# Row and column attention over a 128x192 map: attention times V of all twelve heads as one last stage, with V, x and the result moved in rows of 768 bytes

## What is computed

```
n    = group_norm(x)                        # 32 groups of 6 channels, over the whole map
sw   = softmax over rows of (n[row 0] Wq_s) . (n Wk_s)      # a weight per row, column and head
Q    = n Wq * scale * sw ;  K = n Wk ;  V = n Wv
QK   = einsum('rihd,rjhd->hij', Q, K)       # 192 x 192 per head, summed over rows and d
attn = softmax(QK, axis=j)                  # masks are applied before both softmaxes
out  = x + einsum('hij,rjhd->rihd', attn, V)
```

## Time and profile before

| | |
|---|---|
| median of 3 runs | 582.6 us (578.11 to 585.08) |
| profiled execution, span | 583.2 us |
| busy: PE / DVE / ACT / POOL | 516.6 / 394.4 / 313.4 / 243.0 us |
| mean granted TensorE clock | 0.947 |
| DMA | 183447 packets, 134.30 MB, 230 GB/s over the span |
| packets under 512 bytes | 168224 |

### The profile page before, as it was taken

The page is one execution under the profiler, slowest core; times in us unless marked ns, Lnnn a source line. Parts: engine busy times, 40 slices in busy tenths (PEclk is TensorE's granted clock), DMA queues, the critical chain, the costliest instruction groups (busy, mean ns, idle before and its releaser), DMA issues.

```text
span 583.2 us, 13858 instructions
## 1 busy us (share of the span) xinstructions
PE 516.6 (89%) x5167; PEld 390.0 (67%) x5167; DVE 394.4 (68%) x989; ACT 313.4 (54%) x646; POOL 243.0 (42%) x280
## 2 busy tenths in 40 slices
PE   7697685799999999999899996694999979999893
PEld 5687542355555555455499985494999979998783
DVE  3599767577878777778836686372467663667873
ACT  4477665597999999995412130332456650223231
POOL 2000231755777777774300033572455660002583
PEclk9898899699999999999999999698899998999997
DMA  8997012444666666787699999988777739999998
GB/s 327 384 417 268 2 55 108 163 145 128 217 217 218 215 202 209 200 211 161 120 286 270 269 297 312 320 226 246 256 254 251 258 96 241 303 286 278 309 258 230
DMA packets 183447, 134.30 MB, mean 230 GB/s; under 512 B 168224, under 2 KB 170080, under 8 KB 183392
## 3 DMA queue, kind: packets, MB, share of 16 engines
q1 hardware_dynamic: 132384, 113.80, 63.2%
q10 hardware_dynamic: 51008, 19.76, 13.3%
HBM read 76.92 MB, written 56.62 MB: 229 GB/s over the span
## 4 chain that ended last, share of the span: by engine, by line
PE 68%; DVE 14%; DMA 7%; POOL 3%; ACT 2%; ACTq 2%; issue 2%; SPq 1%; POOLq 0%; DVEq 0%
PE PS L1175 23%; PE PS L1183 13%; PE PS L1271 7%; DVE EXTRA L765 5%; DMA EXTRA<-in_x 4%; PE PS L1301 3%; PE PS L1305 3%; PE PS L1304 3%; PE PS L1303 3%; PE PS L1302 3%; DVE BIG L1040 3%; ACTq L739 2%; POOL BIG L514 2%; DMA out_x<-EXTRA 1%; PE PS L1136 1%
## 5 line engine op out<-in xcount | busy, mean ns | idle before, releaser
L1175 PE MATMUL PS<-WP,EXTRA 128*128 128x384 f16 (+1 forms) x1152 | 159.9, 291 | 8.0 <-DMA EXTRA<-xt_scratch 8.0
L1175 PEld LDWEIGHTS PS<-WP,EXTRA 128*128 128x128 f16 x1152 | 99.3, 99 | 54.9 <-issue 18.8
L514 POOL TENSOR_TENSOR BIG<-BIG,EXTRA 64x512 f32<-64x512 f32 x36 | 45.1, 1265 | 135.6 <-DVE BIG L1040 111.7
L1271 PE MATMUL PS<-BIG,EXTRA 128*128 128x256 f16 x768 | 89.5, 280 | 12.4 <-ACT EXTRA L745 12.4
L471 POOL TENSOR_TENSOR EXTRA<-BIG,EXTRA 128x512 f16<-128x512 f32 x69 | 81.3, 1180 | 42.4 <-ACT EXTRA L578 34.4
L1271 PEld LDWEIGHTS PS<-BIG,EXTRA 128*128 128x128 f16 x768 | 76.4, 100 | 24.7 <-issue 13.2
L1183 PE MATMUL PS<-WP,EXTRA 64*128 64x384 f16 (+1 forms) x1152 | 90.5, 288 | 0.9 <-DVE EXTRA L904 0.9
L477 POOL TENSOR_TENSOR BIG<-EXTRA,BIG 128x192 f16<-128x192 f32 x96 | 53.6, 559 | 49.4 <-ACT BIG L636 49.4
L1183 PEld LDWEIGHTS PS<-WP,EXTRA 64*128 64x128 f16 x1152 | 44.6, 95 | 30.1 <-issue 18.9
L745 ACT ACTIVATE EXTRA<-PS,small 64x512 f32<-64x512 f32 x48 | 31.3, 682 | 60.8 <-PE PS L1271 19.9
L1040 DVE SCALAR_TENSOR_TENSOR BIG<-PS,small,BIG 128x512 f32<-128x512 f32 x72 | 48.9, 738 | 20.5 <-PE PS L1271 20.5
(11 more groups left out here) (177 smaller groups left out, 953.3 us busy)
## 6 DMA issues: line engine op xcount, KB each, us to landing
EXTRA<-in_x SPq DMA_DIRECT2D x28, 768.0 KB, 8.5
xt_scratch<-EXTRA SPq DMA_DIRECT2D x24, 768.0 KB, 3.4
EXTRA<-xt_scratch SPq DMA_DIRECT2D x24, 768.0 KB, 4.3
v_scratch<-EXTRA SPq DMA_DIRECT2D x32, 384.0 KB, 3.9
BIG<-v_scratch SPq DMA_DIRECT2D x16, 768.0 KB, 6.7
BIG<-in_x SPq DMA_DIRECT2D x12, 768.0 KB, 9.5
out_x<-BIG ACTq DMA_DIRECT2D x12, 768.0 KB, 6.4
v_scratch<-EXTRA SPq DMA_DIRECT2D x32, 192.0 KB, 3.9
```

The lines of the kernel that those rows point to most:

```text
L514: pool.tensor_tensor(o, o, OLOW[j % 3][0:E1, :].rearrange("p (r e) -> p r e", r=RI), ALU.add).then_inc(s_lo[h], 1)
L1175: ins = mm(outs[a], xt[:, t, s, q * P:(q + 1) * P], WP[:, t, w, wc], start=first and j == 0, stop=last and j == 2, skip_group_check=True)
L1271: ins = mm(po[:, :, a, :], stationary, moving, start=j == 0, stop=j == len(terms) - 1)
```

## The change

Attention times V is no longer done per half. PE's order becomes: logits of half 0, second projection, logits of half 1, and then one stage of 96 parts over eight tiles and six pairs of heads each. The attention matrices of all twelve heads are kept (`AT` has 12 instead of 6). DRAM scratch for V holds all heads side by side, so a tile's V is 12288 bytes and 6144 bytes for each of 128 partitions. Rows of x and of the result are 192 float32, 768 bytes. V, x and the result lie in "units" (`V_AT`, `X0_AT`, `X1_AT`), most of them in `BIG`; the 64-partition part of x uses partitions 0 to 63 for even tiles and 64 to 127 for odd ones. All loads and all stores of the stage are issued by SP. V's stores in the first projection become one per chunk for 16 chunks and two per chunk for eight.

The diff, cut to its core:

```diff
-    v1_dram = nc.dram_tensor("v1_scratch", [2, 2, E1, R, EH], fp16, kind="Internal").ap()
+    v0_dram = nc.dram_tensor("v0_scratch", [P, R, 2 * E], fp16, kind="Internal").ap()
+    v1_dram = nc.dram_tensor("v1_scratch", [2, E1, R, E], fp16, kind="Internal").ap()
 
...
+                return EXTRA[:, at_units + (at + 5) * UNIT:at_units + (at + 5 + n) * UNIT]
+            return BIG[:, at * UNIT:(at + n) * UNIT]
+
+        V_AT = (-5, 2, 7, 14, 19, -5, 2, 7)
+        X0_AT = (-2, 5, 10, 17, 22, 0, 5, 19)
+        X1_AT = (0, 12, -2, 14)
+        V0 = [units(at, 2).bitcast(fp16).rearrange("p (r s e) -> p r s e", s=2, e=E) for at in V_AT]
+        V1 = [units(at + 2, 1).bitcast(fp16).rearrange("p (r e) -> p r e", e=E) for at in V_AT]
+        XO = [(units(X0_AT[n], 2).rearrange("p (r e) -> p r e", e=E),
+               units(X1_AT[n // 2], 2)[(n % 2) * E1:(n % 2 + 1) * E1].rearrange("p (r e) -> p r e", e=E))
+              for n in range(NRC)]
...
-                    if c < P // CI:
-                        sp.dma_start(v0_dram[h, c * CI:(c + 1) * CI, :, :].rearrange("i r s -> r i s"),
-                                     VS[c % 2][:, :, h, :, :].rearrange("p i s e -> p i (s e)")
-                                     ).then_inc(s_vs[c % 2], 16)
-                    else:
-                        j0 = c * CI - P
-                        for k in range(2):
-                            sp.dma_start(v1_dram[h, k, j0:j0 + CI, :, :].rearrange("i r s -> r i s"),
-                                         VS[c % 2][:, :, h, k, :]).then_inc(s_vs[c % 2], 16)
+                if c < P // CI:
+                    sp.dma_start(v0_dram[c * CI:(c + 1) * CI, :, :].rearrange("i r s -> r i s"),
+                                 VS[c % 2].rearrange("p i s e -> p i (s e)")).then_inc(s_vs[c % 2], 16)
+                else:
+                    j0 = c * CI - P
+                    for k in range(2):
+                        sp.dma_start(v1_dram[k, j0:j0 + CI, :, :].rearrange("i r s -> r i s"),
+                                     VS[c % 2][:, :, k, :]).then_inc(s_vs[c % 2], 16)
...
-            for h in range(2):
-                if h:
-                    for k in (6, 7):
-                        sp.wait_ge(s_out[k], 32)
-                    for b in range(2, 4):
-                        load_xt(b, b)
-                    with sp.Fori(1, TURNS) as t:
-                        for b in range(4):
-                            sp.wait_ge(s_pj[1], (4 * t + b - 3) * 2)
-                            load_xt(4 * t + b, b)
-                    sp.wait_ge(s_pj[1], NG1)
-                load_x(h, 6)
-                load_x(h, 7)
-                for n in range(NV):
-                    sp.wait_ge(s_qk[h], n + 1)
-                    load_v(h, n)
-                    load_x(h, n)
-                for n in range(NRC - NV):
-                    sp.wait_ge(s_av[h], 2 * closes[n] + 2)
-                    load_v(h, n + NV)
-            for k in range(NRC):
-                sp.wait_ge(s_out[k], 64)
...
+            def load_x(n, t):
+                cols = slice(P, C) if t else slice(0, P)
+                sp.dma_start(XO[n][t], xs[rows(n), cols, :].rearrange("r i e -> i r e")).then_inc(s_xl[t][n], 16)
+
+            def store_out(n):
+                sp.wait_ge(s_ad, 2 * HP * (n + 1) - 1)
+                sp.dma_start(outs[rows(n), 0:P, :].rearrange("r i e -> i r e"), XO[n][0]).then_inc(s_out[0][n], 16)
+                sp.wait_ge(s_lo, HP * (n + 1))
+                sp.dma_start(outs[rows(n), P:C, :].rearrange("r i e -> i r e"), XO[n][1]).then_inc(s_out[1][n], 16)
+
+            with sp.Fori(1, TURNS) as t:
+                for b in range(4):
+                    sp.wait_ge(s_pj[1], (4 * t + b - 3) * 2)
+                    load_xt(4 * t + b, b)
+            sp.wait_ge(s_pj[1], NG1)
+            load_v(0)
+            load_x(0, 0)
+            sp.wait_ge(s_qk[1], 1)
+            load_x(0, 1)
+            load_x(1, 1)
+            sp.wait_ge(s_qk[1], 2)
+            load_v(1)
+            load_x(1, 0)
+            sp.wait_ge(s_qk[1], 3)
+            load_v(2)
+            load_x(2, 0)
+            sp.wait_ge(s_qk[1], 4)
+            load_x(2, 1)
+            load_x(3, 1)
+            sp.wait_ge(s_qk[1], 5)
+            load_v(3)
+            load_x(3, 0)
+            sp.wait_ge(s_qk[1], 6)
+            load_v(4)
+            load_x(4, 0)
+
+            store_out(0)
+            sp.wait_ge(s_av, 2 * HP)
+            load_v(5)
+            store_out(1)
+            sp.wait_ge(s_av, 2 * HP * 2)
+            load_v(6)
+            sp.wait_ge(s_out[0][0], 16)
+            load_x(4, 1)
+            load_x(5, 1)
+            store_out(2)
+            sp.wait_ge(s_av, 2 * HP * 3)
+            load_v(7)
+            for n in range(2):
+                sp.wait_ge(s_out[1][n], 16)
+            load_x(5, 0)
+            sp.wait_ge(s_out[0][1], 16)
+            load_x(6, 0)
+            store_out(3)
+            sp.wait_ge(s_av, 2 * HP * 4)
+            load_x(6, 1)
+            load_x(7, 1)
+            store_out(4)
+            sp.wait_ge(s_av, 2 * HP * 5)
+            load_x(7, 0)
+            for n in range(5, NRC):
+                store_out(n)
+            for n in range(NRC):
+                sp.wait_ge(s_out[0][n], 16)
+                sp.wait_ge(s_out[1][n], 16)
 
         @block.gpsimd
         def _(pool):
...
+                attention_low(h, HALF - 2)
+
+            def add_attended(m):
+                (n, hp), t = BLOCK[m // 2], m % 2
+                if hp == 0:
+                    dve.wait_ge(s_xl[t][n], 16)
+                rows = slice((n % 2) * E1, (n % 2 + 1) * E1) if t else slice(0, P)
+                dve.wait_ge(s_av, m + 1)
+                o = XO[n][t][:, :, hp * 2 * D:(hp + 1) * 2 * D]
+                v.scalar_tensor_tensor(o, PS[rows, attended_bank(m), :].rearrange("p (r e) -> p r e", r=RI),
+                                       mxb[rows, WV:WV + 1], o, ALU.mult, ALU.add).then_inc(s_ad, 1)
+
+            dve.wait_ge(s_ql[0], NG0)
+            for k in range(2):
+                dve.wait_ge(s_vs[k], v_stored(NCH - 2 + k))
+            for b in range(2):
+                v.memset(LG[b][E1:P, 1, :], 0.0)
+            softmax_of_heads(0)
+            evacuate1(0, 0)
+            normalise_logits(0, HALF - 1)
+            for g in range(1, 8):
+                if g == 6:
+                    attention_low(0, HALF - 1)
+                evacuate1(0, g)
...
-                    with pe.Fori(1, TURNS) as t:
-                        project1(t)
-
...
+            def wait_for_banks1(t, g):
+
+                if not isinstance(t, int):
+                    pe.wait_ge(s_kvl[1], 8 * t + g - 3)
+                elif t == 0 and g < 3:
+                    when(pe, s_lr[0], (0, HALF - 1, HALF)[g])
+                elif t == 0:
+                    pe.wait_ge(s_kvl[1], g - 2)
+                elif g == 3:
+                    pe.wait_ge(s_atl[0], HALF)
+                else:
+                    pe.wait_ge(s_kvl[1], (7, 8, 6)[g] if g < 3 else 8 * t + g - 3)
...
+            logits(0)
+            project1(0)
+            project1(1)
+            with pe.Fori(2, TURNS) as t:
+                project1(t)
+            logits(1)
+            for m in range(2 * NB):
+                if m == TRANSPOSED_AT:
+                    transposes(1, HALF - 1)
+                attended(m)
```

492 lines of the change are left out of this document (233 added, 259 removed).

## The result

| | before | after |
|---|---|---|
| median | 583.2 us (578.11 to 585.08, 4 runs) | 597.2 us (591.98 to 600.46, 4 runs) |
| ratio after/before | | 1.026, 95% interval 1.018 to 1.034 |
| profiled execution, span | 583.2 us | 590.3 us |
| DMA | 183447 packets, 134.30 MB | 98200 packets, 134.32 MB |

What follows compares the result with a forecast made beforehand. The prediction took PE and DMA as both near their limits, with DMA setting the new end: 412.5 us to the projection's end + 2.0 idle + 173.3 of transfers + 5.4 of loss = 593.2, forecast 593 us, range 565 to 607.

Steps and rivals of the forecast that it cites:

- Up to the second projection: Kernel start to the end of half 0's logits: fewer V stores save ACT's wait, 1.0 us, so it ends at 334.7 us.
- The second projection: 24 chunks at 73.9 us, 0.9 for the sixth head's transposes, 3.0 for new PE waits; end at 412.5 us.
- Logits of half 1: After the second projection: start 3.2 us later, behind POOL, and take 46.0 us, to 461.7.
- PE alone: Attention times V if DMA kept up: 48 head pairs in 83.9 us, 8.4 behind PE, kernel end at 554.9 us.
- The stage by DMA: V, x and results from 412.5 us on: 2.0 us idle, 173.3 of transfers, 5.4 of loss; end at 593.2 us.
- The price of 64 partitions: Loads and stores on 64 partitions in the DMA stage: 215 GB/s, so 12.6 MB take 58.5 us.
- the line through 384 and 6144 bytes: DMA stage, 128 partitions: 768-byte rows put between 325 and 410 GB/s, at 366, so 25.2 MB take 68.8 us.
- the loss of 5.4 us: DMA stage: extra time on 37.7 MB of loads, scaled from 3.8 us seen before, taken to go with the number of transfers.
- SP's single queue adds nothing: DMA stage: all loads and stores in SP's queue cost no extra time, as a transfer is always ahead; size 0.
- The faster one: Rival for the DMA stage: 768-byte rows move like long ones, 146 to 155 us, kernel at 565 us; chance 0.28.
- The much slower one: Rival: one queue in order at 291 GB/s, stage 194.5 us, kernel 609; or 768-byte rows bring nothing, 603; chance 0.22.
- The signs: What the changed profile would show: projection times, DMA share near 1, PE's stage over 95 us, x's rates, idle slices.

Runs made afterwards that it cites:

- e4: The changed kernel with every load of x for the residual cut to the first of its 16 rows: 565.3 us, stage 154.1 us.
- e2: The changed kernel with x of columns 128 to 191 loaded by 8 rows on 128 partitions instead of 16 on 64: 584.2 us, stage 167.9 us.
- e11: A separate kernel of transfers only, no computation, fourteen phases one behind the other, executed once: some 205 GB/s on either half, 372 or 373 for a load beside a store.
- e3: The changed kernel with each load of x and each store split into two transfers of 384-byte rows: 603.1 us, stage 191.2 us.
- e1: The changed kernel with the stores of the result issued by ACT instead of SP: 584.9 us, stage 171.5 us.

## Why the prediction was right, point by point

The forecast was 593 us (range 565 to 607); the median measured is 597.2. The sum itself ends at 593.2 us on the time axis of a profile; the profiled execution ends at 590.3. Its mechanism, DMA and not PE sets the end, is shown by e4: with 17.7 MB left out the stage is 25.9 us shorter. What the change lost by was in good part another thing than the sum had, the order of SP's queue. That its largest term agrees within 1 us is in part luck, as told below.

- **Up to the second projection: 334.7 forecast, 331.2 measured.** ACT's wait for V's store is gone, and the bound of 1.7 us was nearer than the 1.0 taken. The rest of the 4.5 us lies in the earlier part: in its first 100 us the profiled execution had a clock of 0.96, before 0.93, which no step of the change explains.
- **The second projection: 77.8 us forecast, 79.1 measured.** PE's new waits in the first turn were put at 3.0 us. The view of waits of after (total, times, longest) has 3.1:

```profile
PE PS L1240 <- DVE BIG L1020: 1.7, 1, 1.7
PE PS L1232 <- DVE BIG L1020: 1.4, 2, 0.8
```

  Its end came at 410.3 us, forecast 412.5.
- **Logits of half 1: 3.2 + 46.0 us forecast, 3.2 + 44.5 measured**, at a clock of 1.00 instead of 0.96.
- **PE alone: 554.9 us forecast.** From the end of the projection that is 142.4 us; e4's stage took 154.1, with 90.4 us for the head pairs instead of 83.9, and 16.0 behind PE instead of 8.4. The term was up to 11.7 us too small (part of it are stores that queue in e4). It did not matter, as DMA's end was later.
- **The stage by DMA: 180.7 us forecast, 180.0 measured.** The price of 64 partitions is right: 174 to 236 GB/s in the trace, and e2 puts 12.1 us on half of these transfers, forecast by difference 12.8. The 366 GB/s for 128 partitions is not: one direction shows 328 in after and 326 in e11, and the line through 384 and 6144 bytes does not hold at 768 for a single load. With e11's rates for one direction, 327 and 205 GB/s, and V as forecast the stage would be 2.0 + 77.1 + 61.5 + 46.0 = 186.6 us, an estimate, already without the loss of 5.4 us. It took 6.6 us less, which fits the short stretches in which loads and stores overlap in after too, at some 370 GB/s. So a rate that no single direction has and a loss taken for another reason met the right number. e3 gives the price of row length, together with that of 32 more transfers, as 11.2 us of stage, forecast 10.1.
- **"SP's single queue adds nothing": wrong as a statement on the kernel.** There were few idle slices, as the prediction said, and yet 8.5 us of stage came back when the stores left SP's queue. The step looked only for pauses. What it missed is that one queue in order runs most loads and stores one behind the other, and side by side they move more: 372 GB/s on the same half where each alone has some 205 (e11), and near 370 in e1 where after had 303 in the mean. The sum hid this, as its rates were read from transfers that ran one at a time. The Trainium skill ("DMA: Bandwidth & Descriptors", section "Issuing engines are not separate DMA queues") says that issuing from several engines saves only the time of issue. The run with V in ACT's queue agrees (0.8 us); the run with the stores there does not (8.5 us of stage, with DMA as busy as before).
- **The rivals.** The faster one asked for 260 GB/s and more on 64 partitions, which no load or store alone showed. The much slower one asked for 291 GB/s in the stage; measured 316. Its reason, one queue in order, was a real cost all the same, of the size of the loss.
- **The signs.** Three of those named failed though the forecast held. The second projection was to start at 334 to 336 us and end at 411 to 416; it started at 331.2 and ended at 410.3, so by the prediction's own words the first part failed, if by 2.8 us at most. x on 128 partitions was to show 350 to 380 GB/s; it showed 328. Idle slices between a store and the next load were to speak for the in-order queue; there were few, and its cost was there. PE's stage of over 95 us (116.0) with waits for DMA, and 64 partitions near 200 to 230 GB/s (174 to 236), came as named.
- **The Trainium skill** ("SBUF — State Buffer", section "Door 1: The DMA port swizzle (why `[64,N]` ≈ `[32,N]`)") gives partitions 0 to 63, and 64 to 127 alike, eight of sixteen ports and about 218 GB/s. The runs agree for one direction (some 205 on either half); a load beside a store on the same half moved 372. The rule of 512 bytes in the Trainium skill ("DMA: Bandwidth & Descriptors", section "Specifications") would have made this change a gain; here single loads move the same at 384 and 768 bytes (319 to 334 GB/s), and e3 shows a price for the stage in all, 6% of its length.
